# Self-attention queries and keys of a two-layer decoder: turned head by head for each sequence, or packed for four sequences and spread by DMA

## What is computed

```
q, k, v = x @ Wq, x @ Wk, x @ Wv            # 16 heads of 8 numbers each
q = layernorm(q, per head) * gq + bq        # over the 8 numbers of a head
k = layernorm(k, per head) * gk + bk
x = x + softmax(q @ k^T, causal) @ v @ Wo + bo
x = x + local attention over ctx (|i-j| <= 64; queries = norm of x, keys = values = ctx) @ W_proj + b_proj
x = x + quantised linear of norm(x)
```

## Time and profile before

| | |
|---|---|
| median of 3 runs | 1456.49 us (1454.46 to 1458.66) |
| the profiled execution | 1459.37 us, of which 1457.6 us span |
| first phase | 0 to 775 us |
| second phase | 795 to 940 us |
| third phase | 940 to 1457.6 us; its first and last (128th) row maximum start at 941.33 and 1422.39 |
| TensorE busy, granted clock | 89% of the span, 0.972 |
| VectorE, ScalarE, GpSimd busy | 74%, 72%, 43% |

### The profile page before, as it was taken

One profiled execution on the slowest core, in us unless ns is written; L12 is line 12 of the kernel. 1 busy time (PEld: TensorE's weight loads), 2 busy tenths in 40 slices (PEclk: granted clock), 3 DMA queues, 4 the chain that ended last, 5 costly groups with the idle time before them and its releaser, 6 DMA issues.

```text
span 1457.6 us, 42538 instructions
## 1 busy us (share of the span) xinstructions
PE 1294.8 (89%) x15257; PEld 942.1 (65%) x15257; DVE 1081.9 (74%) x2573; ACT 1049.3 (72%) x2841; POOL 633.9 (43%) x844
## 2 busy tenths in 40 slices
PE   4358999999999999999984999889889989999995
PEld 1125676666666666767674999856656666676664
DVE  6998889999899988876665344466668778686665
ACT  2128999999999999999981566647666766766653
POOL 0012424353444434310215554448675776655663
PEclk9999999999999999999995999979999999999997
DMA  6942242413214241020112332220101010000000
GB/s 145 242 121 57 52 102 53 113 49 95 66 48 100 52 108 49 16 94 2 52 35 66 101 96 75 96 84 22 32 10 42 11 41 11 26 25 4 25 11 16
DMA packets 83579, 89.00 MB, mean 61 GB/s; under 512 B 15792, under 2 KB 72752, under 8 KB 78768
## 3 DMA queue, kind: packets, MB, share of 16 engines
q1 hardware_dynamic: 77424, 77.10, 20.3%
q0 software_dynamic: 4096, 8.40, 2.0%
q10 hardware_dynamic: 1856, 0.79, 0.2%
HBM read 64.76 MB, written 17.83 MB: 57 GB/s over the span
## 4 chain that ended last, share of the span: by engine, by line
PE 60%; DVE 13%; ACT 10%; issue 8%; POOL 5%; DMA 2%; ACTq 0%; another core or an unknown queue 0%; DVEq 0%; SPq 0%; POOLq 0%
PE P L796 7%; PE P L958 7%; PE P L2114 5%; PE P L1579 4%; PE P L1612 4%; PE P L814 3%; PE P L940 3%; ACT pr L1019 3%; PE P L917 3%; PE P L928 3%; PE P L912 3%; PE P L2176 2%; PE P L2132 2%; PE P L835 2%; PE P L2069 2%
## 5 line engine op out<-in xcount | busy, mean ns | idle before, releaser
L2433 DVE TENSOR_REDUCE mx<-P 128x8 f32<-128x1024 f32 x128 | 156.5, 1223 | 123.8 <-PE P L2114 85.3
L1019 ACT ACTIVATE pr<-P,nm 128x256 f32<-128x256 f32 x512 | 238.6, 499 | 5.9 <-DVE nm L1217 5.7
L2326 ACT ACTIVATE et<-P 128x1024 f32<-128x1024 f32 x128 | 131.0, 1024 | 122.6 <-PE P L2121 110.2
L1217 DVE TENSOR_REDUCE nm<-P 128x4 f32<-128x1024 f32 x128 | 156.1, 1219 | 25.9 <-PE P L796 23.5
L796 PE MATMUL P<-kt_w,qt 64*128 64x256 f32 x1024 | 145.2, 402 | 4.6 <-ACT pr L1019 4.6
L1001 ACT COPY ptS<-P 128x512 f32<-128x512 f32 x256 | 138.1, 598 | 8.7 <-PE P L814 8.4
L992 ACT ACTIVATE pr<-pr,ri 128x256 f32<-128x256 f32 x254 | 119.6, 536 | 24.6 <-DVE pr L1190 24.0
L704 POOL TENSOR_TENSOR kv_qk<-kv_qk,mixing 128x512 f32<-128x512 f32 x48 | 61.0, 1271 | 151.9 <-DVE pr L1190 151.9
L1675 ACT ACTIVATE hT<-P,mixing 128x128 f32<-128x128 f32 x284 | 81.0, 368 | 61.1 <-PE P L1579 56.8
L698 POOL TENSOR_TENSOR kv_qk<-kv_qk,r_w 128x512 f32<-128x512 f32 x48 | 61.0, 1270 | 145.6 <-DVE pr L1190 100.0
L1019 ACT ACTIVATION_READ_ACCUMULATOR pr<-P,nm 128x1 f32 x512 | 118.2, 231 | 0.0
(11 more groups left out here) (351 smaller groups left out, 3652.4 us busy)
## 6 DMA issues: line engine op xcount, KB each, us to landing
kv_qk<-scr_v SPq DMA_DIRECT2D x16, 1024.0 KB, 8.0
r_w<-scr_r SPq DMA_DIRECT2D x16, 1024.0 KB, 10.8
xt<-scr_xs SPq DMA_DIRECT2D x71, 64.0 KB, 1.8
scr_ys<-yt SPq DMA_DIRECT2D x71, 64.0 KB
x<-in_x SPq DMA_DIRECT2D x8, 256.0 KB, 10.2
scr_v<-mixing SPq DMA_DIRECT2D x8, 256.0 KB, 2.5
scr_r<-mixing SPq DMA_DIRECT2D x8, 256.0 KB, 2.0
xb<-in_x SPq DMA_DIRECT2D x8, 256.0 KB, 3.3
```

The costliest lines, as they stand in the source:

```text
L1019: e = nc.scalar.activation(pr[:, s % 3, h * KEYS:(h + 1) * KEYS], scores(s)[:, h // 2, (h % 2) * KEYS:(h % 2 + 1) * KEYS], ACT.Exp, bias=n ...
L1217: nc.vector.tensor_reduce(nm[:, s % 3, 0:4].rearrange("p (a h) -> p a h", a=2), scores(s).rearrange("p a (h k) -> p a h k", k=KEYS), AX.X, ...
L2326: nc.scalar.activation(et[:, u % 4, :, :, :], scoresT, ACT.Exp).then_inc(S["h_exp"], 1)
L2433: nc.vector.tensor_reduce(mx[:, n % 2, 8 * r:8 * r + 8].rearrange("p (k a) -> p k a", k=2), scores, AX.X, ALU.max, negate=True).then_inc(S ...
```

## The change

Queries and keys are kept packed. The columns of `wqk` (a new copy of the centred weights) are ordered so that column 32*j + 4*c + a holds number c of head 4a+j. The norm then works in place on `qkv` (`normed`), with no padded copy. The transposition of one sequence's keys is one 128 x 128 piece, so four sequences fill bank 7 in one use, and ScalarE copies them to `packed`. Four DMAs on SyncE's queue (`spread_heads`) then write `packed`'s 128 rows to the padded layout. `kt0` to `kt3` become one use `kt`, `qt0` to `qt3` one use `qt`; an `e` use turns one piece instead of four, is read at 128 x 128 to `packedE` and spread by four DMAs too. The products become two uses of bank 7 (`qk0`, `qk1`, two sequences each) instead of four in half of bank 4, and `wo` and the addition no longer wait for their copies. The scores read 8 rows of each strip and the turned scores 9, instead of 32. TensorE waits for the spread (`in_sd0`, `in_sd1`, `in_se`) where it waited for ScalarE. At the start of the third phase one 1 MB copy (`xnE<-qS`) goes away; the weights' scales come in 16 small DMAs instead of 4.

```diff
-        "dxt": -25, "bias": -25, "qk0": -24, "qk1": -23, "qk2": -22, "qk3": -21, "square": -21, "v": -19, "reduce": -20,
-        "guess": -19, "inv0": -18, "inv1": -16, "kn": -14, "qn": -13,
-        "qp": None, "kt0": -13, "qt0": -12, "kt1": -11, "kt2": -7, "qt2": -6, "qt1": -5, "kt3": -2, "qt3": -1}
+        "dxt": -25, "bias": -25, "qk0": -23, "qk1": -22, "square": -21, "v": -19, "reduce": -20,
+        "guess": -19, "inv0": -18, "inv1": -16, "norm0": -14, "norm1": -13,
+        "kt": -12, "qt": -11}
...
-        "dxt": 1, "bias": 7, "qk0": None, "qk1": None, "qk2": None, "qk3": None, "qp": 2, "square": 2, "v": 3,
-        "reduce": 3, "guess": 3, "inv0": 4, "inv1": 4, "kn": 5, "qn": 6,
-        "kt0": 6, "qt0": 7, "kt1": 7, "qt1": 8, "kt2": 9, "qt2": 10, "kt3": 11, "qt3": 12},
+        "dxt": 1, "bias": 7, "qk0": 2, "qk1": 2, "square": 2, "v": 7,
+        "reduce": 3, "guess": 3, "inv0": 4, "inv1": 4, "norm0": 5, "norm1": 5,
+        "kt": 5, "qt": 6},
...
-                **{62 + 2 * b: ("kt", b) for b in range(GS)}, **{63 + 2 * b: ("qt", b) for b in range(GS)}}
+                62: ("kt", 0), 63: ("qt", 0)}
+FRONT_SPREAD = 69
...
-MIDDLE = (("qt0", 1), ("kt3", 1), ("qt3", 1), ("kt1", 2), ("kt2", 2), ("qt0", 3), ("kt1", 3), ("kt3", 3), ("qt2", 3),
-          ("qt3", 3), ("qt2", 2), ("e2", 7))
+MIDDLE = (("qk0", 1), ("qt", 1), ("kt", 3))
...
+        def normed(qkv, g, k, y3):
+
+            x = qkv[:, g % 2, 2 * k:2 * k + 2, :].rearrange("p b (j c a) -> p (b j) a c", c=DH, a=4)
+            nc.vector.tensor_tensor(x, x, bcast(y3[:, 16 * k:16 * k + 16, :], 2, DH), ALU.mult).then_inc(S["d_qkn"], 1)
+
+
+        def spread_heads(sp, dst, src, cols, sem):
+
+            for j in range(4):
+                sp.dma_start(dst[32 * j:32 * j + DH, :, cols], src[32 * j:32 * j + 32, cols]).then_inc(S[sem], 16)
...
-                for dst, src in ((vE, vD), (xnE, qS)):
-                    sp.dma_start(dst[:, :, :, :], src[:, 1]).then_inc(S["in_g"], 16)
+                sp.dma_start(vE[:, :, :, :], vD[:, 1]).then_inc(S["in_g"], 16)
...
+                    for k, (name, dst) in enumerate((("kt", kTd), ("qt", qTd))):
+                        g = self_at(s, name)
+                        if g is not None:
+                            if g >= 2:
+                                sp.wait_ge(S["h_st"], SELF_AT[g - 2] + 8)
+                            sp.wait_ge(S["h7_read"], filled(name, g))
+                            spread_heads(sp, dst[g % 2], packed[:, k, :], slice(0, N), f"in_sd{g % 2}")
+                    for b in range(GS):
+                        g = local_at(s, f"e{b}")
+                        if g is not None:
+                            if g:
+                                sp.wait_ge(S["h_st"], LOCAL_AT[g - 1] + 2 * b + 2)
+                            sp.wait_ge(S["h7_read"], filled(f"e{b}", g))
+                            if g or b:
+                                sp.wait_ge(S["in_se"], local_spread(g, b) - 64)
+                            spread_heads(sp, qTe, packedE, slice(b * T, (b + 1) * T), "in_se")
...
-                        cols, part = slice(b * T, (b + 1) * T), slice(64 * r + 32 * k, 64 * r + 32 * k + 32)
+                        cols, part = slice(b * T, (b + 1) * T), slice(64 * r + 32 * k, 64 * r + 32 * k + DH)
...
                         if local:
-                            pe.wait_ge(S["h7_read"], filled(f"e{b}", g))
+                            pe.wait_ge(S["in_se"], local_spread(g, b))
                             pe.wait_ge(S[f"in_kt{g % 2}"], key_loads(g))
-                        elif g:
-                            pe.wait_ge(S["h7_read"], max(filled(f"{name}{b}", g) for name in ("kt", "qt")))
+                        else:
+                            pe.wait_ge(S[f"in_sd{g % 2}"], self_spread(g))
...
-                        if qk_before[s + 1]:
-                            pe.wait_ge(S["qk_read"], qk_before[s + 1])
...
+                def products(s, middle):
+                    for k in range(2):
+                        g = self_at(s, f"qk{k}")
+                        if g and ((f"qk{k}", g) in MIDDLE) == middle:
+                            bank7_free(f"qk{k}", g)
+                            pe.wait_ge(S["h7_read"], filled("dxt", g))
+                            for i in range(2):
+                                b = 2 * k + i
+                                m = nc.tensor.matmul(bank7[:, 256 * i:256 * i + 256], xTd[:, b * T:(b + 1) * T], wqk[:, :],
+                                                     start=True, stop=True)
+                            m.then_inc(S["h7"], 1)
```

More of the change, by code:

```diff
@@ L138 @@
               "e0": -4, "e1": -2, "e2": 0, "e3": 2, "ft_eps0": 15, "ft_nm0": 16}
[L140 to L143 removed]
+BANK7_H = ("dxt", "qk0", "qk1", "v", "kt", "qt", "e0", "e1", "e2", "e3", "ft", "fmm")
+MIDDLE = (("qk0", 1), ("qt", 1), ("kt", 3))
 FIRST_H, LAST_H = -2, UNITS_H + 21
@@ L1938, in queries, with self_spread, local_spread @@
                 return qTe if local else qTd[g % 2]
-            def queries_turned(name, g):
-                return max(filled(f"{name}{b}", g) for b in range(GS))
+            def self_spread(g):
+                return 16 * 8 * (g // 2 + 1)
+            def local_spread(g, b):
+                return 16 * 4 * (GS * g + b + 1)
             def head_at(r, t, j):
@@ L2097, in operands @@
                             pe.wait_ge(S["e_xn"], GS * g + b + 1)
-                            turn(bank7, quads(xnE[:, b])).then_inc(S["h7"], 1)
+                            nc.tensor.transpose(bank7[:, b * T:(b + 1) * T], xnE[:, b, :], ident[:, :]).then_inc(S["h7"], 1)
+                def products(s, middle):
+                    for k in range(2):
+                        g = self_at(s, f"qk{k}")
[7 more added lines that the diff above has]
+                            m.then_inc(S["h7"], 1)
                 def maxima(n):
@@ L2155, in tensor_program @@
                                 m.then_inc(S["h_st"], 1)
+                    products(s, True)
                     operands(s, True)
@@ L2224, in tensor_program @@
                                          stop=True).then_inc(S["h_wo"], 1)
-                    g = self_at(s, "qp")
-                    if g is not None:
-                        bank7_free("qp", g)
-                        pe.wait_ge(S["h7_read"], filled("dxt", g))
-                        for b in range(GS):
-                            m = nc.tensor.matmul(P[:, 7 - b // 2, b % 2 * 256:b % 2 * 256 + 256], xTd[:, b * T:(b + 1) * T],
-                                                 wD[:, 0:256], start=True, stop=True)
-                            if b % 2:
-                                m.then_inc(S[("h7", "p_qp")[b // 2]], 1)
+                    products(s, False)
                     g = self_at(s, "v")
@@ L2296, in operands, with products @@
                             if g:
-                                act.wait_ge(S["h_st"], LOCAL_AT[g - 1] + 2 * b + 2)
-                            nc.scalar.activation(qTe[:, :, b * T:(b + 1) * T],
-                                                 bank7.rearrange("p (a n) -> p a n", a=4), ACT.Copy,
-                                                 scale=gbs[:, 6:7]).then_inc(S["h7_read"], 1)
+                                act.wait_ge(S["in_se"], local_spread(g - 1, b))
+                            cols = slice(b * T, (b + 1) * T)
+                            nc.scalar.activation(packedE[:, cols], bank7[:, cols], ACT.Copy, scale=DH ** -0.5)\
+                              .then_inc(S["h7_read"], 1)
+                def products(s, middle):
+                    for k in range(2):
+                        g = self_at(s, f"qk{k}")
+                        if g and ((f"qk{k}", g) in MIDDLE) == middle:
+                            got(f"qk{k}", g)
+                            if k == 0 and g > 2:
+                                act.wait_ge(S["h7"], filled("qt", g - 2))
+                            elif k == 0 and g == 2:
+                                act.wait_ge(S["m_fr"], len(FRONT_TURNED))
+                            nc.scalar.copy(qkv[:, g % 2, 2 * k:2 * k + 2, :].rearrange("p b n -> p (b n)"), bank7)\
+                              .then_inc(S["h7_read"], 1)
                 for s in range(FIRST_H, LAST_H):
@@ L2344, in scalar_program @@
                           .then_inc(S["h_ot"], 1)
[L2346 to L2361 removed]
+                    turned_rows(s, False)
+                    products(s, False)
                     g = self_at(s, "v")
```

234 lines of the change are left out of this document (78 added, 156 removed), and 6 rows, old and new, of the table SELF_BY_SLOT.

## The result

The changed kernel takes 1517.37 us (median of 4 runs, 1511.54 to 1521.08) against 1456.65 for the kernel before: ratio 1.0413, 95% interval 1.0377 to 1.0450, some 60 us **slower**. I had forecast 1437. The profiled execution took 1517.21 us, with a span of 1514.8.

A forecast was written before the change was run, and what follows sets the result against it. Bounds: TensorE in the second phase, a loop of scores and maxima at 3.20 us a slot in the third. Terms -2.6 - 6.5 - 11 - 4 + 4 + 1 = -19.1 us took the median 1456.49 to 1437.4; range 1419 to 1455.

The forecast's parts named there:

- The rows do not set the time, and I count nothing for this.: Third-phase scores: reading 8 or 9 rows instead of 32 was counted as no change in time.
- floor pairs: Third phase: pairs of slots bound by the loop of scores and maxima, 6.40 us a pair, unmoved by the change.
- Part 6: Cost of the spreads' DMAs on SyncE's queue: +4 us for contention with maxima DMAs, +1 us for waits at `e3`.
- R1: Rival, slower: spreads hold up the maxima DMAs at the turned scores of every second slot; 1473 us, chance 0.09.
- R4: Rival: a spread's four DMAs run in turn, landing after 10.4 us, so `e3` is late; 1463 us, chance 0.03.
- Part 1: Second phase: 24 fewer turns on a full TensorE save 2.6 us; the first spreads are covered.
- Part 2: Slots 80 to 86 and two like places: 3.0 us won each; slots 53 to 100 win 6.5 us together.
- Part 3: Slots 21 to 53, crowded and 32.1 us over the floor: 11 us won.
- Part 4: Slots 0 to 21, 18.6 us over the floor: 4 us won, bounds 0 and -10.
- Part 5: Slots 100 to 127, lone `e` uses at the floor: no change, 0 us.
- R3: Rival, more gain: the early crowd dissolves and TensorE's clock does not fall in the third phase; 1418 us, chance 0.10.
- R2: Rival, little gain: the excess over the floor is VectorE's and GpSimd's; about -5 us, 1452 us, chance 0.12.

The follow-up runs named there:

- run 2: The changed kernel with its score matmuls reading 32 rows of each strip again, spreads kept whole: 1484.71 us, ratio 1.0207 to the kernel before.
- run 10: The changed kernel with 32-row score reads and every spread cut to 8 bytes a row: 1455.49 us, ratio 1.0018 to the kernel before.
- run 11: The changed kernel with 32-row reads, the queries' spread of groups 3 to 7 delayed and the front's spreads cut in two: 1465.68 us, ratio 1.0090.

## Why the prediction was wrong

In parts of the kernel before's time: narrow reads +2.1% (change against run 2), spreads +1.9% (run 2 against run 10), the rest +0.2% (run 10). Together 4.1% by the unrounded ratios, of which I had forecast nothing for the reads, +0.3% (4 and 1 us) for the spreads and -1.7% for the rest. These are shares in this kernel; in the kernel before, the narrow reads alone cost 1.0%. Of the difference between the change and run 2, some 14 us lie in slots 54 to 56, 70 to 72 and 86 to 88.

- **"The rows do not set the time, and I count nothing for this."** This step failed worst: it put at nothing a term that is worth 2.1%. A score of 8 rows takes as long as one of 32 at full clock (282 and 283 ns), and the floor pairs there are still 6.40 us, as I said. But with fewer rows read the clock falls more often, and more so in this kernel's slots than in the old ones. I had taken a duration from a row at full clock and not asked what keeps it full. The half-rate stretches of the earlier trace rows were the hint, and I used them as something that could be won.
- **Part 6, +4 for contention and +1 for `e3`.** The mechanism was there with its place (R1), its size was not. I spread 0.6 us over 14 bursts; in fact each pair of `kt` and `qt` puts 512 KB around one DMA of the maxima, which costs that slot 3 to 5 us and the clock after it some more. The time of SyncE for a DMA was taken from the key loads (0.36 us) and is 0.70. I had a burst landed 4.0 us after ScalarE's read, and R4 had 10.4; the bursts ahead of slot 94 took 6.7 and 7.9. The 8 us that I worked out from the Trainium skill (DMA: Bandwidth & Descriptors, "Anatomy of one DMA — SWDGE (gpsimd) path") is near that by luck: that figure is for DMAs from GpSimd, and I added four of them. The wait at `e3` itself was small (7.4 us over 16 waits of the weight loads, 0.4 of TensorE's). R1's 1473 was too low as well: it knew neither the clock nor the front.
- **Part 1, -2.6, "covered".** Neither half held. That the first maximum of run 11 starts 2.5 us earlier is no gain of the turns: there the second phase itself begins earlier, at 791.70 for 795.55, and up to the first mask it takes 145.3 us for 144.0 (143.8 to 144.7 in the four traces with the old order). TensorE is busy 2.2 us less, and waits instead. The window of the second phase in the kernel before, then that of run 11 with two waits of TensorE (0.9 us in all before, 4.5 in run 11):

```profile
795.60:939.80 144.20, 143.13 (x1259) 142.40 (x1258) 61.03 (x220) 92.29 (x303) 68.86 (x93) 0.99 0.29 82
```

```profile
791.70:937.20 145.50, 140.92 (x1234) 139.91 (x1234) 61.62 (x216) 88.50 (x297) 70.49 (x94) 0.99 0.29 82
PE P L1601 <- issue: 2.1, 1, 2.1
PE P L1626 <- DVE qkv L1444: 1.7, 1, 1.7
```

And the spreads were not covered. I had asked whether they would be there in time, and not who stands behind them on SyncE's queue: the stores of `yt`, for which VectorE and TensorE wait. In the changed kernel the second phase takes 149.1 us, +5.1.
- **Part 2, -3.0 a place.** Run 10 has 22.6 us from slot 80 to 86 for 24.2, so -1.6: the four slots from 80 win 2.2, and the one from 84, which I held fixed as VectorE's, loses 0.6 to the slower sum of squares. In the changed kernel itself the six slots take 23.6.
- **Part 3, -11.** Run 10 wins 5.4 of it. Slot 34, held up by GpSimd's part of the chain, got longer (10.88 for 8.98). The clock fall around it stands in the trace (1082.1 to 1088.9), but not in the earlier trace rows, which I named for it and where that slice still reads 9.
- **Part 4, -4.** It is +2.2 in run 10, lost in the first slots (0 to 8: 40.2 for 37.2). I take the longer chain of `kt` behind both multiplications, the spread and the products as the reason; no run shows it alone.
- **Part 5, 0.** +1.0 in the changed kernel, near enough; +3.0 in run 10, mostly by slot 112.
- **Slips in the working**, which change no verdict. The slot from 84 to 85 is 1.5 over the floor of 3.20, not 1.3. R1 counts the 1 us of `e3` twice and comes to 1472. R3 says far bounds and takes 8 for part 4, where I had put 10. The 2.60 us called usual for the DMA of the maxima is slow; 1.7 is usual.

With the spreads and reads taken out, **R2** describes the kernel best: the excess was VectorE's and GpSimd's, and TensorE's and ScalarE's savings became waits for them. Even R2's 5 us did not come (run 10: +0.2%).

## What to carry to other kernels

Before you drop TensorE work that looks free, or narrow what its matmuls read, ask what keeps its clock up: the duration in a row of the trace tells the price at the clock of that row only. A burst on a DMA queue is not priced by whether it arrives in time, but by the small DMA or store beside or behind it that somebody waits for; let it go right behind the landing of that one, and count the issue time of each DMA on its queue before cutting it in pieces. And where engines wait for each other in a loop, count each saving as a new wait until a run with the costs removed shows that it is time saved. To credit a stage with a gain, measure it from its own start, not from the start of the program.
